# Other places for the front and back steps in the three tables of quarter slots

## The reference

```python
# L0: one explicit step of a PDE on the 256x256 grid of a sequence, then relu
df = -gradv_Af + gradvv_Bf * 0.5
x = jnp.maximum(f + df * dt[:, None, None], 0.0)
# L1: adapter with a chosen expert, residual, layer norm over the features
hidden = gelu(x @ down_W.T + down_b)
hidden = hidden @ expert_W[idx].T + expert_b[idx] + domain_emb[idx]
x = layer_norm(hidden @ up_W.T + up_b + x) * ln_gamma + ln_beta
# L2: twice silu(scale * whole_norm(.) + shift) and a matmul, residual;
# whole_norm takes mean and variance over all 256x256 numbers of a sequence
out = silu(scale * whole_norm(x) + shift) @ W_in + b_in
x = silu(scale * whole_norm(out) + shift) @ W_out + b_out + x
# L3: modulated norm, attention with 16 heads, an additive bias for every head
# and a mask of keys, then the MLP of 1024
x = _ln(x) * (1.0 + scale3) + shift3
scores = jnp.einsum('bhqd,bhkd->bhqk', q / 4, k) + attention_bias
scores = jnp.where(src_mask, -jnp.inf, scores)
x = x + (merge(softmax(scores) @ v) @ Wo + bo)
h = _ln(x) * g2 + beta2
return x + gelu2(h @ W1 + b1) @ W2 + b2
```

## Time and profile before

| | us |
|---|---|
| median of 3 runs | 944.76 |
| lowest, highest | 942.92, 946.6 |
| the profiled execution | 941.49 |
| its span | 939.7 |
| PE busy | 858.8 (91%) |
| DVE busy | 751.3 (80%) |
| ACT busy | 731.6 (78%) |
| POOL busy | 239.2 (25%) |
| DMA, mean over the span | 139 GB/s |
| granted clock of PE, mean | 0.975 |

### The profile page before, as it was taken

How to read it: one execution, slowest core, us unless ns; L and a number is a source line. 1 busy time by engine, 2 the same in 40 slices (tenths; PEclk the granted TensorE clock), 3 DMA queues, 4 the chain that set the end, 5 groups by cost and what they waited for, 6 DMA issues and landing times.

```text
span 939.7 us, 18088 instructions
## 1 busy us (share of the span) xinstructions
PE 858.8 (91%) x5646; PEld 661.4 (70%) x5731; DVE 751.3 (80%) x2375; ACT 731.6 (78%) x1901; POOL 239.2 (25%) x237
## 2 busy tenths in 40 slices
PE   7675869999999999999999999999999999998987
PEld 6353646777777777777777777777777777776766
DVE  7466788988898889888898888888898889876542
ACT  3123879979798888979798888979798888987773
POOL 1233213222223224222223224222223224120100
PEclk9678899999999999999999999999999999999999
DMA  9814545645446353644446363644447353645500
GB/s 252 246 54 114 173 125 146 177 138 152 114 122 193 102 162 103 191 133 139 127 124 191 103 160 103 193 139 139 121 127 189 106 159 103 179 136 150 154 13 22
DMA packets 133081, 130.88 MB, mean 139 GB/s; under 512 B 18265, under 2 KB 123481, under 8 KB 132969
## 3 DMA queue, kind: packets, MB, share of 16 engines
q1 hardware_dynamic: 101072, 111.49, 42.1%
q10 hardware_dynamic: 31914, 18.23, 6.8%
HBM read 112.61 MB, written 17.07 MB: 138 GB/s over the span
## 4 chain that ended last, share of the span: by engine, by line
PE 48%; ACT 23%; DVE 18%; issue 8%; POOL 1%; DMA 1%; ACTq 0%; DVEq 0%; POOLq 0%
PE ff_ps L1335 11%; PE PT_ps L1371 6%; ACT Pr L1057 5%; PE ff_ps L1316 5%; DVE bias L921 4%; PE ctx_ps L1393 4%; PE G L1216 4%; PE scores_ps L1356 4%; PE G L1139 3%; ACT L1057 3%; ACT tanh L1039 3%; ACT PT L1070 3%; ACT ffT L1043 3%; PE scores_ps L1353 2%; PE G L1212 2%
## 5 line engine op out<-in xcount | busy, mean ns | idle before, releaser
L1057 ACT ACTIVATE Pr<-bias,nmax 128x256 f32<-128x256 f32 x512 | 255.9, 506 | 41.9 <-DVE nmax L921 41.4
L921 DVE CUSTOM_DVE_ANT_0 bias<-scores_ps,bias 128x256 f32<-128x256 f32 x512 | 195.4, 420 | 60.0 <-issue 35.4
L1070 ACT ACTIVATE PT<-PT_ps 128x512 f32<-128x512 f32 x256 | 151.7, 593 | 50.3 <-PE PT_ps L1371 41.0
L1371 PE MATMUL PT_ps<-ident,Pr 128*128 128x128 f32 x1024 | 156.4, 275 | 9.0 <-ACT Pr L1057 9.0
L559 POOL TENSOR_TENSOR rstd<-var,half_neg 128x2 f32<-128x2 f32 (+1 forms) x64 | 42.7, 667 | 403.5 <-DVE var L684 256.4
L1371 PEld LDWEIGHTS PT_ps<-ident,Pr 128*128 128x128 f32 x1024 | 119.8, 141 | 18.4 <-ACT Pr L1057 15.0
L1316 PE MATMUL ff_ps<-ctxT,w 128*128 128x256 f32 x480 | 116.9, 386 | 10.7 <-ACT ffT L1043 8.9
L1335 PE MATMUL ff_ps<-w,ffT 128*128 128x256 f32 x480 | 114.8, 382 | 0.3 <-DVE ffT L898 0.3
L1316 PEld LDWEIGHTS ff_ps<-ctxT,w 128*128 128x128 f32 x480 | 86.3, 190 | 30.2 <-ACT ffT L1043 14.2
L1356 PE MATMUL scores_ps<-k_stack,q_stack 96*128 96x256 bf16 x512 | 99.2, 275 | 6.7 <-issue 3.3
L1057 ACT ACTIVATION_READ_ACCUMULATOR Pr<-bias,nmax 128x1 f32 x512 | 100.8, 197 | 0.0
(11 more groups left out here) (219 smaller groups left out, 1628.6 us busy)
## 6 DMA issues: line engine op xcount, KB each, us to landing
bias<-in_fside_Bx16xSxS_dram SPq DMA_DIRECT2D x256, 256.0 KB, 3.2
part_dram<-front ACTq DMA_DIRECT2D x32, 384.0 KB, 3.5
q_stack<-part_dram SPq DMA_DIRECT2D x32, 192.0 KB, 3.3
k_stack<-part_dram SPq DMA_DIRECT2D x32, 192.0 KB, 3.9
F<-in_x_dram SPq DMA_DIRECT2D x16, 256.0 KB, 3.7
ada<-rows_dram SPq DMA_DIRECT2D x16, 256.0 KB, 4.5
q_stack<-part_dram SPq DMA_DIRECT2D x32, 128.0 KB, 3.6
k_stack<-part_dram SPq DMA_DIRECT2D x32, 128.0 KB, 3.8
```

What stands on the lines that cost most here:

```text
L921: nc.vector.tensor_tensor_reduce(out=t, in0=SP_[:, n % 2, q * S:(q + 1) * S], in1=t, scale=-1.0, scalar=BIG, op0=ALU.add, op1=ALU.min, acc ...
L1057: ins = nc.scalar.activation(Pr[:, n % PR, q, :], bias[:, n // CH % RING, 2 * (n % CH) + q, :], ACT.Exp, bias=nmax[:, n, q:q + 1], scale=-1.0,
L1070: nc.scalar.activation(PT[:, m % BATCH, :, :].rearrange("p c q -> p (c q)"), TP[:, m % 2, :], ACT.Identity).then_inc(pt_ok, 1)
L1371: ins = pe.transpose(TP[:, m % 2, c * S + q * P:c * S + (q + 1) * P], Pr[:, m % PR, q, c * P:(c + 1) * P], ident[:, :])
```

## The change

Only numbers in `AT`, `AT_FIRST` and `AT_LAST` differ (`SP_AT` and `HEAD_AT` don't). Every step is still there on the engine where it was; the instructions are the same, but for loads of activation tables, which depend on the order: 2 fewer of them. Lines of the changed kernel are one higher than those of before. Three entries as an example:

```diff
-            "s_mask": (19.75, 19.75), "s_rows": (14.75, 14.75), "x4": (25.75, 39.25), "s_fill": (9, 9),
-            "s_bq": (10.25, 10.25), "s_w2": (34.25, 34.25), "prods_p": (0, 10), "prods": (2, 4.5),
-            "diffs": (3.5, 9.5), "edges": (3.5, 11), "l0": (2.5, 16.25), "x1": (5, 20.5), "relu": (2.25, 14),
+            "s_rows": (10.5, 10.5), "x4": (25, 45.75), "s_fill": (8.75, 8.75), "s_bq": (16.25, 16.25),
+            "s_w2": (34.75, 34.75), "prods_p": (3.25, 7.75), "prods": (2, 2), "diffs": (3.75, 11.25),
+            "edges": (4.75, 14.5), "l0": (1.75, 15), "x1": (4.75, 17.25), "relu": (0.75, 10.25),
```

More of the change, by code:

```diff
@@ L72 @@
            "masks": 0}
-AT = {"x4": (28.75, 45.25), "ctx_spread": (18, 36.25), "ctx": (19.75, 36.5), "ctx_scale": (19.25, 36.25),
[4 rows of a table removed]
[L78 to L81, removed]
[6 rows of a table removed]
-      "k_split": (26, 41.5), "k_out": (26, 41.25), "v": (28.75, 45.75), "V": (30.75, 45), "mask": (20, 2)}
@@ L89 @@
-AT_FIRST = {"s_trig": (0, 0), "s_onehot": (1.5, 1.5), "s_grid": (0.25, 0.25), "s_h1": (0.25, 0.25),
-            "s_h2": (5.5, 5.5), "s_h2t": (7, 7), "s_sel": (0.25, 0.25), "s_cond": (7.5, 7.5), "s_condt": (8.5, 8.5),
-            "s_mask": (19.75, 19.75), "s_rows": (14.75, 14.75), "x4": (25.75, 39.25), "s_fill": (9, 9),
-            "s_bq": (10.25, 10.25), "s_w2": (34.25, 34.25), "prods_p": (0, 10), "prods": (2, 4.5),
-            "diffs": (3.5, 9.5), "edges": (3.5, 11), "l0": (2.5, 16.25), "x1": (5, 20.5), "relu": (2.25, 14),
[9 rows of a table removed]
@@ L103 @@
-AT_LAST = {"ctx_spread": (20.25, 52.75), "ctx": (20.25, 37), "ctx_scale": (20.25, 42), "wo": (21.5, 41.25),
[4 rows of a table removed]
-           "w2": ((31, 34.25, 47.25, 47.5), (59, 61.25, 68.25, 77)), "out": (54.75, 76), "store": (57.25, 63)}
+AT = {"x4": (30.5, 45), "ctx_spread": (19, 36.25), "ctx": (19.75, 36.25), "ctx_scale": (19.75, 36.25),
[4 rows of a table added]
+      "w2": ((31.25, 33, 33, 35.25), (46.75, 46.75, 48.5, 51.25)), "out": (35.75, 51), "store": (48, 60.75),
+      "prods_p": (1.25, 15.25), "prods": (0.75, 12.5), "diffs": (2.75, 16), "edges": (2.75, 16.25),
+      "l0": (4.75, 18.5), "x1": (5.5, 18), "relu": (5.25, 18.5), "x1_turn": (7.5, 20), "x1T": (7, 20),
+      "res1": (9, 23.75), "down": (8, 21.5), "hid": (8.25, 20.25), "expert": (9.25, 22.25), "expT": (8.5, 21),
[7 rows of a table added]
+      "mask": (20, 2)}
@@ new lines @@
+AT_FIRST = {"s_trig": (0.5, 0.5), "s_onehot": (1.25, 1.25), "s_grid": (2, 2), "s_h1": (0.5, 0.5), "s_h2": (5, 5),
+            "s_h2t": (5.75, 5.75), "s_sel": (0.5, 0.5), "s_cond": (7, 7), "s_condt": (8.75, 8.75), "s_mask": (19, 19),
+            "s_rows": (10.5, 10.5), "x4": (25, 45.75), "s_fill": (8.75, 8.75), "s_bq": (16.25, 16.25),
+            "s_w2": (34.75, 34.75), "prods_p": (3.25, 7.75), "prods": (2, 2), "diffs": (3.75, 11.25),
[10 rows of a table added]
+AT_LAST = {"ctx_spread": (17, 46.75), "ctx": (20, 37.25), "ctx_scale": (20.75, 51), "wo": (21.5, 37.25),
[4 rows of a table added]
+           "w2": ((31.5, 36.25, 38.75, 45.25), (52.5, 58, 75, 77.25)), "out": (62.5, 74.75), "store": (61.5, 62.5)}
```

## The result

Over 22 runs of each the changed kernel took 946.07 us (943.29 to 948.84) and the kernel before 943.57 us (941.48 to 947.27): a ratio of 1.0021, with a 95% interval of 1.0011 to 1.0031, that is 2.0 us slower (the two medians differ by 2.5). The forecast was 10.2 us slower. The profiled executions differ by more than the medians, 946.23 against 941.49 us, as that of the kernel before is among the shortest of its runs; the part on the hardware says where they spread.

The account below looks back on a forecast made before the run. TensorE's queue was taken to bound middle turns, and one nearly slack-free chain the prologue. Terms 11.2 + 0 − 2 + 0.5 + 0.5 = +10.2 us on the median 944.8 gave 955.0 us, range 949 to 961.

Parts of the forecast that it names:

- 1. prods.1 ahead of diffs.0: Prologue, DVE: diffs.0 and edges.0 wait behind prods.1 for F, so l0.0 starts at 32.3 instead of 22.77; +9.5 us.
- 2. TensorE in the same chain: Prologue: s_h2t ahead of x1_turn.0 +0.5, s_cond ahead of expert.0 +1.5, stat0.0 no longer behind s_cond's copy −1.35 us.
- rival (b): Prologue and turn 0: the shift is partly absorbed by a sooner clock rise, turn 0 and exps.0; −4, 951; chance 0.12.
- 3. s_rows ahead of the warming: Prologue, TensorE: s_rows waits for cond, w_in.0 starts later, +1.6; l0.1 loses the turning, −0.5; together +1.1 us.
- 4. The first heads: ACT: y1.1 ahead of head 0 saves two table loads but delays exps.0; booked 0, range −1 to +1 us.
- 5. Turn 0: TensorE's waits for stat0.0's moments and for y0.0 shrink; −2 us, range 0 to −3.1.
- 6. Turns 1 to 6: Middle turns: waits for the PT copy and h1 keep their cause, two moves cost something; +0.5 us, range 0 to +5.
- rival (c): Middle turns: both waits, 1.6 us a turn, vanish through DVE moves; −9.7 in six turns, 945.3; chance 0.05.
- The two costs that I had weighed there: Turns 1 to 6: k_out.0 later on ACT delays stack loads, 0 to 0.8 us; x4.1 on GpSimd runs beside hn.1.
- rival (a): Each turn pays: hn.1 stretches by 1.95 us in six turns, stack loads land late; +5, 960; chance 0.12.
- 7. Turn 7: Turn 7 and end: h1[2].0 ahead of copy_pt.25 and exps.27 makes ACT wait for w1[2].0; +0.5 us, range 0 to +1.
- The sign that I had set for being wrong: Wrong if l0.0 starts before 30, or turn 0's end difference isn't about the run's end difference.

Follow-up runs that it names:

- e14: e13 with aff1, y1 and w_out of b = 1 in AT_FIRST as before, behind the first head; 932.5 us, ratio 0.9886.
- e1: The kernel before with only AT_FIRST of the changed kernel; ratio 1.0062, +5.9 us.
- e6: The kernel before with two entries of AT changed, y0 of b = 0 to 12 and w_in of b = 0 to 14; ratio 0.9909, −8.6 us.
- e7: The changed kernel with y0 of b = 0 in AT back from 12 to 11.5; ratio 1.0082 to the kernel before, +7.7 us.
- e2: The kernel before with only AT of the changed kernel; ratio 0.9916, −7.9 us.
- e3: The kernel before with only AT_LAST of the changed kernel; ratio 1.0013, +1.2 us.
- e5_prods_only: The kernel before with only prods of b = 1 in AT_FIRST moved ahead of diffs.0 and edges.0; ratio 1.0083, +7.8 us.
- e9: The kernel before with e6's moves and matmuls of no use, 8 ahead of avg1.0 and 4 ahead of q.0; ratio 0.9899, −9.5 us.
- e13: The changed kernel with prods.1 put back, s_grid ahead of s_onehot, old AT_LAST, and e9's 12 matmuls of no use; 932.75 us, ratio 0.9888.

## Why the prediction was wrong

By the steps of the prediction:

**1. prods.1 ahead of diffs.0, +9.5: right.** l0.0 started 9.05 us later; alone the move cost 7.8 us, and taking it back in the changed kernel gave 9.9.

**2. TensorE in the same chain, +0.5 + 1.5 − 1.35: sign wrong.** From x1.0 to up.0 the chain took 8.15 us before and 6.97 in the changed kernel, −1.2 instead of +2.0. s_cond was priced at the 3.3 us of its row at half the clock. Placed behind s_h2 and down.0 it ran at 2.4 GHz in 1.9 us, which hid behind hid.0 (from the end of down.0 to expert.0 it is 1.81 us in both kernels); the 1.2 us come from x1_turn.0, down.0 and expert.0, which ran at the faster clock too. I had the faster clock as part of rival (b), and should have put it into the sum: a step that moves keeps its duration only if it keeps its clock. The −1.35 of stat0.0 was right (from up.0 to stat0.0 7.56 before, 6.24 after).

**3. s_rows ahead of the warming, +1.1: right (+1.0).** From stat0.0 to w_in.0 6.1 us before, 8.0 after (+1.9, booked +1.6); from w_in.0 to w_out.0 0.9 less (booked −0.5), as l0.1 ran at the faster clock. At the first scores 8.2 us stood instead of 11.2, at the first head 8.66, below the 102.5 to 105.5 us that I had named for it (100.64); q.0 at half the clock (3.78 us against 1.99) worked against the gains there.

**4. The first heads, 0: right as far as it could be measured** (e14). exps.1 came 7.2 us later than before, and l0.0 of pair 1 6.5 us.

**5. Turn 0, −2: measured −1.1.** The two waits did what was booked: the one at avg0.0 fell from 3.61 to 2.62 us (2.3 forecast) and the one for y0.0 from 1.80 to 0.70. Against this stands what `AT_FIRST` costs in turn 0 (99.3 us in e1 against 97.8), whose cause stays open.

**6. Turns 1 to 6, +0.5 booked, −5.4 measured: this step failed.** I wrote that the wait of `times_v` for the copy keeps its cause, "as those steps keep their places against each other", and in rival (c) that ACT's order ahead of it is as before. It isn't: y0.0 had moved by one slot, which is named as a move, but I looked at it only for the time of y0.0 itself, and read the ACT order as a sum of busy times, which is unchanged. The position of the table load was not looked at. The runs showed in its place: with y0.0 behind exps.12 the load back stands behind copy_pt.11, which comes 1.5 us sooner in the turn, the wait of 0.83 us is gone and each turn is 0.9 us shorter (e6); with y0.0 put back the gain is gone (e7).

Rival (c) held this very wait at 0.83 us a turn, with a chance of 0.05. Its 945.3 us came near the measured 946.07, but that is luck: it had both waits vanish (−9.7 us) through moves on DVE, and only one vanished, through the move on ACT.

The two costs that I had weighed there came and cost nothing that the runs show: e6, which has neither move, and e2, which has both, have turns of the same length (104.66 to 104.78 and 104.66 to 104.68 us). k_out.0 was issued 2.2 us later in the turn of pair 5, but SP's loads of the stacks followed it 2.8 us behind instead of 4.4, and so went out 9.6 us ahead of the next pair's first `bias_and_max` instead of 10.2, 0.6 us later and not the 3.4 booked. That they went out at 711.2, the very 711 of the forecast, is luck, as the whole turn stood 3.0 us later by then. hn.1 took 2.70 us beside x4.1 in each turn, as it did in turn 7 before. The changed kernel on DVE, for the earlier trace rows:

```profile
638.59 2.70 DVE L665 TENSOR_SCALAR ffT<-x,back_mv,back_rstd 128x256 f32<-128x256 f32 x2
```

and on POOL:

```profile
638.52 1.27 POOL L605 TENSOR_TENSOR x<-front,ada 128x512 f32<-128x512 f32 x1
```

What I had overlooked: in the kernel before it was x4.0 that ran beside hn.0 in each middle turn and stretched it, and the change moved x4.0 away as well. hn.0 of pair 2, before and after:

```profile
371.29 1.69 DVE L664 TENSOR_SCALAR ffT<-x,back_mv,back_rstd 128x256 f32<-128x256 f32 x2
```

```profile
376.55 0.73 DVE L665 TENSOR_SCALAR ffT<-x,back_mv,back_rstd 128x256 f32<-128x256 f32 x2
```

So DVE paid 1.0 us a turn for both, not the 1.95 of rival (a).

**7. Turn 7, +0.5: short of the measured +2.6.** The order costs 0.9 us, within the 0 to 1 given, and in two of six profiles, the changed kernel's among them, a lower clock costs 1.7 more, which the term didn't hold.

Taken together: the largest term was right to half a microsecond at its place. The two profiles differ by 4.7 us, 5.5 less than the 10.2 booked: 5.9 less in turns 1 to 6 and 2.5 less up to the first head, but 0.9 more in turn 0 and 2.1 more in turn 7. Up to the 2.0 us of the runs it is another 2.7, as the profiled execution of the kernel before is one of the shortest of its runs. The sign that I had set for being wrong came: 7.5 us at the end of turn 0, 4.7 at the end of the run.

## What to carry to other kernels

A move of one step in an in-order queue also moves what is attached to it, here the load of an activation table: find where the load back falls, and who waits for what stands behind it. A gain that repeats in each turn deserves a look at every wait of the engine that bounds the kernel, by name, before any single cost at the start is added up: 0.9 us in each of six turns paid for more than half of a delay of 9 us. And when a step moves to another neighbourhood on TensorE, price it at both levels of the clock.

## What the runs showed of the hardware

Kernels with the same order in the prologue reached the first head at 92.0 (before), 98.1 (e2), 96.2 (e3) and 92.9 us (e6) in their profiled executions. Of the spread, l0.1 and q.0 at the one or the other level of the clock are the parts that can be read off: q.0 took 1.99 us in the kernel before and 3.78 in the other three, l0.1 took 4.8 us in the kernel before, 5.8 in e2 and e3, and 3.3 in e6. The middle turns of one kernel agreed within 0.25 us in all profiles. So in these profiles the spread is made in the first 100 us, and a difference of two profiles' spans is worth less than the difference of their turns.

The runs without a profile fit this. The kernel before ran 62 times beside the experiments: the 16 executions with a mean granted clock of 0.966 or less took 946.7 us on average (944.7 to 949.0), the 14 with 0.974 or more took 941.4 us (940.1 to 942.9).

In the prologue the mean granted clock between 50 and 75 us was 0.74 to 0.86 in the profiles without extra matmuls in that chain, but for the 0.66 of e5_prods_only, and 0.91 to 1.00 in the three with them (e9, e13, e14).
